# A Mamba-2 layer and a gated FFN: the FFN's row copy behind the next tile's tanh, and squares and an output projection at other places

## The chip, the cores and the metric

The kernel runs on one core of a Trainium2 chip. The metric is device microseconds of one launch, weights' preparation included: the median of three runs, and beside it one execution that was profiled.

## The reference

Input x is (4, 512, 512): four sequences ("batches") of 512 tokens. All weights are float32 inputs.

```
xn  = layernorm(x)
out = x + (xn + mamba2(xn)) + ffn(xn)

mamba2: z, xBC, dt = split(xn @ w_in)            # 1024, 1280, 16 columns
        xBC = silu(causal_conv4(xBC) + conv_b);  X, B, C = split(xBC)
        dt  = softplus(dt + dt_bias);  A = -exp(A_log)
        y   = ssd(X*dt, dt*A, B, C) + X*D        # state space, 16 heads of 64
        y   = y * silu(z)
        y   = y * rsqrt(mean(y*y) + eps) * norm_w
        return y @ w_out
ffn:    hidden = fwht(silu(xn @ W1.T) * (xn @ W3.T))   # 2048 wide, Hadamard
        return hidden @ W2.T
```

## The kernel before

**Precision.** Each product of the large projections is three float16 matmuls (high part by high part, high by low, low by high), summed in PSUM in float32. A weight tile is scaled by a power of two from its sum of squares and split into parts: ScalarE writes the high part (`split_hi`, line 924), VectorE the low part (`split_lo`, line 1194). In batch 0 this happens while the tiles are used, and the parts are stored to HBM; batches 1 to 3 load them.

**Tiles.** A batch has 50 weight tiles, each 12 matmuls of 128x512 on TensorE: ten C (conv inputs), eight Z (gate z), and sixteen pairs A(i), U(i), the FFN's gate and linear rows. For A, ScalarE takes a tanh from PSUM and VectorE makes `hs` from it (line 1260). For U, VectorE multiplies `hs` by the tile in PSUM (line 1265), ScalarE copies the result as float16 to `hid_hi` (line 978), and GpSimd subtracts that copy from `hs` for `hid_lo` (line 1443). After the tiles come sixteen steps G(i), which multiply hidden by W2; in batch 0 also H(i), which prepare W2.

**Quarters.** The state-space part runs over four quarters c of 128 tokens, as steps put between the tiles. T: transposes and the product B by C on TensorE; Xdt on VectorE (1339); on GpSimd x times D (`XD`, 1464) and Xdec (1468). ES: decay differences, on ScalarE (1059) for half of the heads, on GpSimd (1454, 1458) for the others. X: their exponentials on ScalarE (1072, 1074) and the product with `Gm` on VectorE (1348). S: state products on TensorE (782), the new state's matmul from Xdec (788), t1 on VectorE (1353), its sum with XD and the state's decay on GpSimd (1495, 1497). R: state sum on VectorE. Y: diagonal matmuls (796), y's sum and gate on VectorE (1365, 1368), and y's square with its row sum on ScalarE (1083). N, Q, V: scale, column sums and mean of y's squares; yh, yl. ROW: reciprocal root on GpSimd. W: output projection, 24 matmuls (line 600 with `wo_hi`, `wo_lo`), into PSUM bank 3 for quarters 0 to 2.

**Order.** There is one list per batch, `SCHEDULES[b]`, made by `make_schedule` from `FIRST`, `FIRST_AT` and `STEP_FIRST` for batch 0, and from `FRONT` and `STEP_AT` for the others. An entry of a step is the number of FFN tiles (A and U counted) that stand ahead of it. All five engines walk this one list and issue, in order, what their branch has for an item, so an engine that waits holds up all its later items. Copies, tanhs and products wait on semaphores of one count per tile or quarter.

**Weight scales in batch 0.** The FFN's weights are scaled in eight quads of four tiles. SQ takes the quad's squares on ScalarE in two halves (line 1008), QS sums them over the partitions on TensorE (739, 740, columns 2 and 3 of bank 3) and makes the scale on VectorE (`to_scale`, 1172 to 1178, 1308). WOQ, WOS and WOH are the same for w_out: squares (1033), sum and scale (644, 1330), high parts (1037) and low parts (1333). F transforms W2's blocks (719) and copies them out (1015).

The lines ahead of the change at its main place, on ScalarE:

```python
else:                                   # U
    if i == 0:
        act.wait_ge(w2_used.sem, w2_used.at(b, -1))
    act.wait_ge(evac.sem, evicted(b, key))
    nc.scalar.activation(hid_hi[:, i, :], hs[i % 2], ACT.Copy).then_inc(hid_h.sem, 1)
```

## Time and profile before

| | before |
|---|---|
| median of 3 runs (lowest, highest) | 968.58 us (967.49, 969.43) |
| profiled execution, its own time | 965.39 us |
| span from first to last instruction | 963.6 us |
| TensorE busy | 934.7 us, 97% |
| VectorE, ScalarE, GpSimd busy | 555.8, 391.4, 276.1 us |
| copy of U's rows, line 978 | 64 of 629 ns |
| subtract on GpSimd, line 1443 | 64 of 1113 ns |
| mean granted clock of TensorE | 0.996 of 2.4 GHz |
| chain that ended last | TensorE 67% |

TensorE's matmuls are pipelined: one of 128x512 in float16 is listed with 379 ns, but the next starts 0.216 us later, so a tile takes 2.6 us. An idle time is listed in front of the instruction that ended it, with the releaser that came last. Batch 0 lies before 301.6 us of the span, batch 1 before 522.6, batch 2 before 743.8.

### The profile page before, as it was taken

To read this page: it belongs to the slowest core of one execution; us is meant where nothing else is said; L and a number is where in the kernel's file an instruction comes from. 1 tells how busy PE (TensorE), PEld (TensorE's weight loads), DVE (VectorE), ACT (ScalarE), POOL (GpSimd) and SP (SyncE) were. 2 spreads that over 40 slices of the span, in tenths; PEclk is the share of its full clock that TensorE was granted. 3 is DMA by queue.
4 is the path that set the end of the run, shared out by engine and by line. 5 is a ranking of instruction groups with operands and counts; after the bars stand their busy time and mean duration, and the time that the engine had idled before them with its cause. 6 is when DMAs were issued, how large, how long until landed. Compare 5 with 4: busy or idle time off the path is not lost.

```text
span 963.6 us, 13435 instructions
## 1 busy us (share of the span) xinstructions
PE 934.7 (97%) x5000; PEld 469.3 (49%) x5000; DVE 555.8 (58%) x955; ACT 391.4 (41%) x690; POOL 276.1 (29%) x354
## 2 busy tenths in 40 slices
PE   9899987989899999999999999999999999999998
PEld 4444443545344445555454445555445445555543
DVE  7876588875534756556532766566451666575421
ACT  6678874533323445233221434233222444343200
POOL 0000446352000116466110106565210104654410
PEclk9999999999999999999999999999999999999999
DMA  9798355434224335525223435436223435256123
GB/s 336 247 349 295 112 192 193 131 124 137 96 74 147 125 111 159 155 72 176 88 67 113 143 99 164 145 97 175 78 76 101 143 107 160 65 151 153 45 77 98
DMA packets 76208, 134.26 MB, mean 139 GB/s; under 512 B 7536, under 2 KB 20464, under 8 KB 74096
## 3 DMA queue, kind: packets, MB, share of 16 engines
q1 hardware_dynamic: 56640, 104.88, 34.1%
q10 hardware_dynamic: 19504, 28.53, 10.0%
q8 instruction: 40, 0.66, 0.3%
q14 instruction: 24, 0.20, 0.1%
HBM read 107.43 MB, written 25.95 MB: 138 GB/s over the span
## 4 chain that ended last, share of the span: by engine, by line
PE 67%; DVE 1%; DMA 1%; ACT 1%; issue 0%; DVEq 0%; ACTq 0%
PE ps L600 46%; PE ps L834 14%; PE ps L796 2%; PE ps L782 1%; PE ps L788 1%; PE ps L768 1%; DMA arena<-cs_rows 1%; PE ps L619 0%; PE ps L638 0%; PE ps L751 0%; PE ps L771 0%; DVE arena L1348 0%; DVE arena L1426 0%; ACT arena L1059 0%; DVE arena L1265 0%
## 5 line engine op out<-in xcount | busy, mean ns | idle before, releaser
L600 PE MATMUL ps<-xh,arena 128*128 128x512 f16 x1592 | 487.9, 379 | 3.4 <-DVE arena L1194 3.3
L600 PE MATMUL ps<-xl,arena 128*128 128x512 f16 x796 | 302.0, 379 | 0.0
L600 PEld LDWEIGHTS ps<-xh,arena 128*128 128x128 f16 x1592 | 158.3, 99 | 190.3 <-issue 5.9
L834 PE MATMUL ps<-arena 128*128 128x512 f16 x768 | 171.1, 379 | 0.0
L1443 POOL TENSOR_TENSOR arena<-arena 128x512 f16<-128x512 f32 x64 | 71.2, 1113 | 334.6 <-ACT arena L978 334.6
L1244 DVE SCALAR_TENSOR_TENSOR arena<-ps,cw,arena 128x511 f32<-128x511 f32 (+2 forms) x120 | 89.4, 747 | 66.9 <-ACT arena L968 65.0
L600 PEld LDWEIGHTS ps<-xl,arena 128*128 128x128 f16 x796 | 77.9, 98 | 88.7 <-issue 3.3
L834 PEld LDWEIGHTS ps<-arena 128*128 128x128 f16 x768 | 74.1, 98 | 91.2 <-issue 5.5
L978 ACT ACTIVATE arena<-arena 128x512 f16<-128x512 f32 x64 | 40.2, 629 | 141.3 <-DVE arena L1265 141.3
L1260 DVE SCALAR_TENSOR_TENSOR arena<-arena,ps 128x512 f32<-128x512 f32 x64 | 44.0, 687 | 77.3 <-ACT arena L973 77.0
L600 PE MATMUL ps<-wo_hi,arena 128*128 128x512 f16 x256 | 79.9, 384 | 3.6 <-DVE wo_lo L1333 3.4
L973 ACT ACTIVATE arena<-ps,f 128x512 f32<-128x512 f32 x64 | 43.4, 678 | 85.0 <-PE ps L600 85.0
L1454 POOL TENSOR_TENSOR arena<-arena 128x1024 f32<-128x1024 f32 x16 | 30.7, 1920 | 112.5 <-DMA arena<-cs_rows 112.5
L1265 DVE SCALAR_TENSOR_TENSOR arena<-ps,arena 128x512 f32<-128x512 f32 x64 | 44.1, 689 | 24.6 <-PE ps L600 23.3
L1348 DVE TENSOR_TENSOR arena<-arena 128x2048 f32<-128x2048 f32 x16 | 40.5, 2528 | 19.9 <-ACT arena L1074 19.9
L600 PE MATMUL ps<-wo_lo,arena 128*128 128x512 f16 x128 | 49.3, 385 | 0.0
L600 PEld LDWEIGHTS ps<-wo_hi,arena 128*128 128x128 f16 x256 | 25.3, 99 | 37.1 <-DVE wo_lo L1333 3.9
L1059 ACT ACTIVATE arena<-arena 128x128 f32<-128x128 f32 x128 | 40.5, 389 | 5.8 <-DMA arena<-cs_rows 5.8
L1194 DVE SCALAR_TENSOR_TENSOR arena<-arena,scl 128x512 f16<-128x512 f32 x50 | 38.7, 778 | 5.8 <-ACT arena L924 5.8
L924 ACT ACTIVATE arena<-arena,scl 128x512 f16<-128x512 f32 x50 | 35.3, 711 | 12.8 <-DVE f L1308 5.9
L968 ACT ACTIVATE arena<-ps,cb,cw 128x512 f32<-128x512 f32 x40 | 30.8, 771 | 23.1 <-PE ps L600 22.1
L1426 DVE SCALAR_TENSOR_TENSOR arena<-ps,f_w,arena 128x512 f32<-128x512 f32 x16 | 10.9, 745 | 50.3 <-PE ps L834 50.3
(179 smaller groups left out, 1092.8 us busy)
## 6 DMA issues: line engine op xcount, KB each, us to landing
arena<-w_parts SPq DMA_DIRECT2D x198, 256.0 KB, 2.6
w_parts<-arena SPq DMA_DIRECT2D x66, 256.0 KB, 2.6
arena<-cs_rows ACTq DMA_DIRECT2D x16, 1024.0 KB, 5.7
arena<-w SPq DMA_DIRECT2D x24, 512.0 KB, 4.9
arena<-ecs_rows ACTq DMA_DIRECT2D x24, 256.0 KB, 6.9
arena<-x ACTq DMA_DIRECT2D x18, 256.0 KB, 3.4
w_mid<-arena SPq DMA_DIRECT2D x8, 512.0 KB, 3.5
arena<-w_mid SPq DMA_DIRECT2D x16, 256.0 KB, 2.6
```

The source lines that it names most:

```text
L600: ins = nc.tensor.matmul(out_ap, lhs(i, a), rhs(i, c), start=(i == 0 and s == 0), stop=(i == n - 1 and s == 2))
L834: ins = nc.tensor.matmul(bank(t), hw[a][:, i, t * P:(t + 1) * P], w2s[i % W2R][:, d, :], start=(i == 0 and s == 0), stop=(i == JF - 1 and ...
L924: nc.scalar.activation(part_hi[p % PARTS], raw_tile(p), ACT.Copy, scale=scl[:, n:n + 1]).then_inc(w_hi.sem, 1)
L973: nc.scalar.activation(slot, src, ACT.Tanh, scale=f_half[:, 0:1] if kind == "Z" else f_13[:, i // 2:i // 2 + 1]).then_inc(tanh_ok.sem, 1)
L978: nc.scalar.activation(hid_hi[:, i, :], hs[i % 2], ACT.Copy).then_inc(hid_h.sem, 1)
L1059: ins = nc.scalar.activation(Eb[:, h, :], csbc[:, h, :], ACT.Relu, scale=-1.0, bias=cs_s[:, c * NH + h:c * NH + h + 1])
L1194: nc.vector.scalar_tensor_tensor(out=part_lo[p % PARTS], in0=raw_tile(p), scalar=scl[:, n:n + 1], in1=part_hi[p % PARTS], op0=ALU.mult, op ...
L1244: ins = nc.vector.scalar_tensor_tensor(out=a[:, s:L], in0=src[:, 0:L - s], scalar=cw[:, i, TAPS - 1 - s:TAPS - s], in1=a[:, s:L], op0=ALU. ...
L1260: nc.vector.scalar_tensor_tensor(out=hs[i % 2], in0=tb[tanh[key] % 2], scalar=1.0, in1=src, op0=ALU.add, op1=ALU.mult).then_inc(evac.sem, 1)
L1265: nc.vector.scalar_tensor_tensor(out=hs[i % 2], in0=src, scalar=HID / (2 * XS * XS), in1=hs[i % 2], op0=ALU.mult, op1=ALU.mult).then_inc(e ...
L1348: nc.vector.tensor_tensor(Eb, Eb, Gm.unsqueeze(1).to_broadcast([P, NH, P]), ALU.mult).then_inc(m_ok.sem, 1)
L1443: nc.gpsimd.tensor_tensor(hid_lo[:, i, :], hs[i % 2], hid_hi[:, i, :], ALU.subtract).then_inc(hid_l.sem, 1)
```

## The change

1. ScalarE's copy of U(i) to `hid_hi` is no longer issued at U(i). It is issued at the next tile, behind that tile's tanh (or behind the conv's first product, if the tile is a C); the copy of the last U stands behind its own tile.
2. In batch 0 the halves of a quad's squares are two items, SQ 2q and SQ 2q+1, most of them at two tiles in a row; quad 6's sum QS moves from 20 to 18 FFN tiles.
3. y's square on ScalarE is an item of its own, YS. In batch 0 it stands a tile after Y for quarters 0, 1 and 3, and at Y's tile for quarter 2; in the others it stands where it was, right behind Y.
4. In batch 0, N and Q of quarter 1 move from 20 to 21 FFN tiles, W of quarter 0 from 18 to 19, so that QS of quad 6 and tile A9 now stand ahead of W0. QS 6 waits on TensorE for V0's read of the mean instead of W0's result, VectorE no longer waits for N1 there, and W0 waits for quad 6's scale (count 7 instead of 6), as both use bank 3.

```diff
-FIRST = ("... C5 F1 SQ0 Z4 F2 C6 F3 QS0 Z5 F4 C7 F5 SQ1 Z6 F6 Z7 F7 QS1 E0 A0").split()
+FIRST = ("... C5 F1 SQ0 Z4 SQ1 F2 C6 F3 QS0 Z5 F4 C7 F5 SQ2 Z6 SQ3 F6 Z7 F7 QS1 E0 A0").split()
...
-            [("SQ", 2, 1), ("QS", 2, 3), ("SQ", 3, 4), ("QS", 3, 7), ("SQ", 4, 8), ("QS", 4, 12), ("SQ", 5, 11), ("QS", 5, 14),
-             ("SQ", 6, 16), ("QS", 6, 20), ("SQ", 7, 20), ("QS", 7, 23)] +
+            [("SQ", n, at) for n, at in enumerate((1, 2, 4, 5, 7, 8, 11, 12, 15, 16, 19, 20), 4)] +
+            [("QS", q, at) for q, at in enumerate((3, 7, 12, 14, 18, 23), 2)] +
...
-              "Y": (9, 17, 26, 34), "N": (12, 20, 28, 37), "Q": (12, 20, 28, 37), "V": (14, 23, 30, 39), "W": (18, 25, 31, 41),
-              "ROW": (15, 24, 31, 40)}
+              "Y": (9, 17, 26, 34), "YS": (10, 18, 26, 35), "N": (12, 21, 28, 37),
+              "Q": (12, 21, 28, 37), "V": (14, 23, 30, 39), "W": (19, 25, 31, 41), "ROW": (15, 24, 31, 40)}
...
     "Y": (6, 14, 22, 32),
+    "YS": (6, 14, 22, 32),
...
                         elif i == 6:
-                            pe.wait_ge(mamba_evac.sem, mamba_evac.at(0, 0))
+                            pe.wait_ge(mean_read.sem, mean_read.at(0, 0))
...
                             pe.wait_ge(wo_l, QE)
-                            pe.wait_ge(scale_13, 6)
+                            pe.wait_ge(scale_13, 7)
...
+                def hidden_hi(key):
+                    i = key[1]
+                    if i == 0:
+                        act.wait_ge(w2_used.sem, w2_used.at(b, -1))
+                    act.wait_ge(evac.sem, evicted(b, key))
+                    nc.scalar.activation(hid_hi[:, i, :], hs[i % 2], ACT.Copy).then_inc(hid_h.sem, 1)
...
-                    else:
-                        if i == 0:
-                            act.wait_ge(w2_used.sem, w2_used.at(b, -1))
-                        act.wait_ge(evac.sem, evicted(b, key))
-                        nc.scalar.activation(hid_hi[:, i, :], hs[i % 2], ACT.Copy).then_inc(hid_h.sem, 1)
+                    if p > 0 and STREAMS[b][p - 1][0] == "U":
+                        hidden_hi(STREAMS[b][p - 1])
...
                         finish((kind, i))
+                        if POS[b][kind, i] == NT - 1:
+                            hidden_hi((kind, i))
...
-                    elif kind == "Y":
+                    elif kind == "YS":
...
-                        if i in (4, 6):
-                            dve.wait_ge(pe_tot.sem, pe_tot.at(0, i // 6))
+                        if i == 4:
+                            dve.wait_ge(pe_tot.sem, pe_tot.at(0, 0))
```

ScalarE's branch for SQ makes one half per item, with the same instruction on the same data as before.

## Rows read from the trace of the kernel before

**Rows 1.** The page, part 1: busy us, share of the span and instructions of each engine.

```profile
PE 934.7 (97%) x5000; PEld 469.3 (49%) x5000; DVE 555.8 (58%) x955; ACT 391.4 (41%) x690; POOL 276.1 (29%) x354
```

**Rows 2.** Busy time by batch: stretch, its us, then each engine, granted clock, DMA share, GB/s.

```profile
0.00:301.60 301.60, 276.32 (x1437) 137.55 (x1438) 200.96 (x398) 169.35 (x299) 71.65 (x96) 0.99 0.56 187
...
301.60:522.60 221.00, 221.00 (x1216) 112.11 (x1216) 121.51 (x198) 76.67 (x136) 68.67 (x87) 1.00 0.40 120
```

**Rows 3.** Timeline of TensorE: start, us, line, operands, then idle before it and its releaser.

```profile
45.08 0.39 PE L600 MATMUL ps<-xh,arena 128*128 128x512 f16 x1 [2.37 <-DVE arena L1194]
...
120.28 0.36 PE L644 MATMUL ps<-row_sq,con 128*128 128x9 f32 x2 [1.27 <-ACT arena L1033]
...
128.88 0.35 PE L739 MATMUL ps<-row_sq,con 128*128 128x2 f32 x2 [3.04 <-issue]
...
138.62 0.38 PE L810 MATMUL ps<-cmean,arena 128*128 128x1 f32 x2 [0.58 <-DVE arena L1372]
...
152.43 1.97 PE L796 MATMUL ps<-arena 128*64 128x128 f32 x32 [2.14 <-DVE arena L1353]
...
160.53 0.50 PE L600 MATMUL ps<-wo_hi,arena 128*128 128x512 f16 x1 [3.43 <-DVE wo_lo L1333]
...
172.59 0.28 PE L739 MATMUL ps<-row_sq,con 128*128 128x2 f32 x2
```

**Rows 4.** Busy time in stretches of 25 us, columns as in rows 2.

```profile
25.00:50.00 25.00, 21.59 (x147) 10.44 (x145) 21.03 (x38) 17.17 (x27) 1.11 (x3) 1.00 0.74 254
...
125.00:150.00 25.00, 21.38 (x107) 12.04 (x105) 21.97 (x48) 20.12 (x37) 13.33 (x12) 0.93 0.42 134
...
150.00:175.00 25.00, 19.43 (x115) 10.15 (x114) 18.59 (x23) 11.97 (x23) 13.54 (x15) 0.93 0.58 190
```

**Rows 5.** Timeline of GpSimd, step T0 of batch 1, then Xdec of batch 2.

```profile
357.62 1.09 POOL L1443 TENSOR_TENSOR arena<-arena 128x512 f16<-128x512 f32 x1 [16.97 <-ACT arena L978]
358.66 1.90 POOL L1464 TENSOR_TENSOR arena<-arena,dcol 128x1024 f32<-128x1024 f32 x1
361.46 1.90 POOL L1468 TENSOR_TENSOR arena<-arena 128x1024 f32<-128x1024 f32 x1 [0.89 <-DVE arena L1339]
...
582.42 1.90 POOL L1468 TENSOR_TENSOR arena<-arena 128x1024 f32<-128x1024 f32 x1 [0.89 <-DVE arena L1339]
```

**Rows 6.** Timeline of TensorE, batch 1: the state matmul.

```profile
364.96 1.88 PE L788 MATMUL ps<-arena 128*128 128x512 f32 x4
```

**Rows 7.** Timeline of ScalarE, batch 1: tanh of Z7.

```profile
358.83 0.69 ACT L973 ACTIVATE arena<-ps,f_half 128x512 f32<-128x512 f32 x1 [1.29 <-PE ps L600]
```

**Rows 8.** Timeline of VectorE, batch 1: product of step X0.

```profile
361.96 3.55 DVE L1348 TENSOR_TENSOR arena<-arena 128x2048 f32<-128x2048 f32 x1 [0.38 <-ACT arena L1074]
```

**Rows 9.** Two lines of VectorE: durations in ns (min/median/max), first and last start.

```profile
L1348 DVE TENSOR_TENSOR arena<-arena x16: 2282/2293/3552, 111.2 to 906.1; 128x2048 f32<-128x2048 f32 x16
...
L1333 DVE SCALAR_TENSOR_TENSOR wo_lo<-arena,nws,wo_hi x8: 739/747/2040, 134.0 to 159.7; 128x512 f16<-128x512 f32 x8
```

**Rows 10.** Timeline of VectorE and of GpSimd, batch 1, one after the other.

```profile
447.86 1.67 DVE L1387 SCALAR_TENSOR_TENSOR arena<-arena 128x1024 f16<-128x1024 f32 x1
...
448.40 2.88 POOL L1464 TENSOR_TENSOR arena<-arena,dcol 128x1024 f32<-128x1024 f32 x1
```

**Rows 11.** Timeline of ScalarE, batch 0: a square and the tanh of A2.

```profile
100.52 1.04 ACT L1008 ACTIVATE arena<-arena 128x1024 bf16<-128x1024 f32 x1
...
105.24 0.67 ACT L973 ACTIVATE arena<-ps,f 128x512 f32<-128x512 f32 x1
```

**Rows 12.** Timeline of TensorE, batch 0: the state matmul.

```profile
107.28 1.10 PE L788 MATMUL ps<-arena 128*128 128x512 f32 x2
```

**Rows 13.** Timelines of GpSimd, ScalarE and VectorE, batch 0, quarter 1.

```profile
134.28 2.34 POOL L1464 TENSOR_TENSOR arena<-arena,dcol 128x1024 f32<-128x1024 f32 x1
...
138.34 0.67 ACT L973 ACTIVATE arena<-ps,f 128x512 f32<-128x512 f32 x1
...
148.87 2.28 DVE L1348 TENSOR_TENSOR arena<-arena 128x2048 f32<-128x2048 f32 x1
```

More of the change, by code:

```diff
@@ L39 @@
 WARM = (32, 8)
-FIRST = ("B G1S C C0 G1N C1 Z0 DT C2 DTL Z1 C3 Z2 C4 SUM Z3 WOL F0 C5 F1 SQ0 Z4 F2 C6 F3 QS0 Z5 F4 C7 F5 SQ1 Z6 F6 Z7 F7 QS1 E0 A0").split()
+FIRST = ("B G1S C C0 G1N C1 Z0 DT C2 DTL Z1 C3 Z2 C4 SUM Z3 WOL F0 C5 F1 SQ0 Z4 SQ1 F2 C6 F3 QS0 Z5 F4 C7 F5 SQ2 Z6 SQ3 F6 Z7 F7 QS1 E0 A0").split()
 FRONT = "CZCCZCZeCZCZeCPCZCZCPZ"
@@ L997, in _ @@
                     elif kind == "SQ":
-                        act.wait_ge(d_quad[i], 32)
+                        quad, half_of = divmod(i, 2)
+                        act.wait_ge(d_quad[quad], 32)
                         if i == 0:
                             act.wait_ge(sq_g1, G1_ACT)
-                        elif i == QUADS_EARLY:
+                        elif i == 2 * QUADS_EARLY:
                             act.wait_ge(xt_done.sem, xt_done.at(0, MC - 1))
-                        junk = sq_act[i >= QUADS_EARLY]
-                        for half_of in range(2):
-                            if i not in (0, QUADS_EARLY):
-                                act.wait_ge(sq_quads, 2 * i + half_of - 1)
-                            column = SQ_Q + 2 * i + half_of
-                            nc.scalar.activation(junk[:, half_of * 2 * TILE:(half_of + 1) * 2 * TILE].rearrange("p (s c) -> p s c", s=2),
-                                                 raw_load_view(i, half_of), ACT.Square,
-                                                 accum_out=row_sq[:, column:column + 1]).then_inc(sq_quads, 1)
+                        if quad not in (0, QUADS_EARLY):
+                            act.wait_ge(sq_quads, i - 1)
+                        junk = sq_act[quad >= QUADS_EARLY][:, half_of * 2 * TILE:(half_of + 1) * 2 * TILE]
+                        nc.scalar.activation(junk.rearrange("p (s c) -> p s c", s=2), raw_load_view(quad, half_of), ACT.Square,
+                                             accum_out=row_sq[:, SQ_Q + i:SQ_Q + i + 1]).then_inc(sq_quads, 1)
                     elif kind == "F":
```

## The prediction

> **What bounds the kernel now.** Read the page's busy line first [rows 1]: TensorE is busy for 934.7 of 963.6 us, VectorE for 555.8, ScalarE and GpSimd for less. So the kernel is a queue of matmuls, and an edit on another engine counts only through TensorE's waits. The second view, busy time by batch [rows 2], says where those waits are: from 301.6 to 522.6, which is batch 1, TensorE is busy for all of 221.00 us (batches 2 and 3 repeat it), while in batch 0 it misses 25.3 us of 301.6. Two things follow. The change can gain only in batch 0; in batches 1 to 3, where the copy is deferred as well, it can only lose. The third view is TensorE's own timeline with the idle time ahead of an instruction [rows 3]: between 116 and 165 us it waits 1.27 us for a square of w_out (WOS), 3.04 for QS4, 0.58 for V0, 2.14 for Y1 and 3.43 for the output projection W0, 10.5 us in all. The granted clock is the fourth [rows 4]: the two stretches of 25 us that hold the 3.04 and the 3.43 us waits have a mean of 0.93, and the one with a 2.37 us wait at 45.08 has 1.00. Between the two levels, 2.4 and 1.2 GHz, a mean of 0.93 is 0.07 x 25 / 0.5 = 3.5 us at the lower one, so each of the two long waits cost 1.7 us more behind it.
>
> **The deferred copy: what it moves.** ScalarE's copy of a gated row block U(i) is now issued behind the next tile's tanh. That tile needs 12 matmuls, 2.6 us, so the copy comes some 2.5 us later, or more where steps stand between the two tiles. ScalarE itself loses nothing. But GpSimd takes its steps in order, and its subtract for U(i) waits for the copy; whatever is queued behind that subtract moves too. In every batch the steps behind U's are T (x times D, then Xdec), ES, ROW and S.
>
> **Batches 1 to 3, step T0.** Before, GpSimd runs the subtract of U1 at 357.62, XD at 358.66 and Xdec from 361.46 to 363.36 [rows 5]; the state matmul that needs Xdec starts at 364.96, without a wait [rows 6]. Now U1's copy comes behind Z7's tanh, which starts at 358.83 and takes 0.69 [rows 7]: the next instruction starts 0.1 before its end, at 359.4, the copy (0.63) ends at 360.05, subtract 360.1 to 361.2 (1.09), XD to 363.1 (1.90), Xdec to 365.0 (1.90). That alone is level with the 364.96 at which TensorE arrives: a loss of 0.0 to 0.1.
> It will not run so smoothly, because VectorE's product for step X0 falls into the same place. In the profile this product waits while Xdec runs: it starts at 361.96, half a microsecond into Xdec, and takes 3.55 us, where the median of its 16 instances is 2.29 [rows 8, 9]. The reverse is in [rows 10]: GpSimd's product, issued at 448.40 while VectorE's L1387 (two operands from SBUF) was running or first in line, took 2.88 instead of 1.90 and ended 1.75 us after L1387 did. So the two exclude each other for whole instructions, and the one that has been waiting goes next. Now ScalarE's exponentials end 0.2 us later (the copy is ahead of them), so the product is issued at 362.1 or 362.2, in the middle of XD (361.2 to 363.1). It gets its turn when XD ends and ends 2.15 us later, as it did behind Xdec (363.36 to 365.51): 365.25. Xdec, issued at 363.05, then waits for it and ends 1.75 later, at 367.0. The state matmul starts at 367.05 instead of 364.96: 2.1 us lost. Batch 2 repeats batch 1 to the hundredth (its Xdec is at 582.42, 220.96 later [rows 5]), and batch 3 likewise, so 3 x 2.1 = 6.3 us. Bounds: 0.0 a batch if there is no collision, 2.6 if a later margin (Xdec of quarter 2, which by the same working comes 0.5 us ahead of its matmul) is used up as well; I take 2.1, as 361.96 and 448.40 are the same two instruction kinds. A wait of 2.1 us is below the 2.37 that left the clock alone.
> The Trainium skill has this exclusion as a rule (SBUF — State Buffer, "Who interferes with whom"): a VectorE instruction with two SBUF inputs and a GpSimd one that reads SBUF hold the shared port for the whole instruction, in order of issue. By that rule the loss is 2.1 us a batch; without an exclusive lock it would be 0.1. The 3.55 us in [rows 8] agree with the rule.
> The rest of batches 1 to 3 I cost at nothing. S1 and S2 also stand behind a U, and their x*D sum arrives for Y1 and Y2 about 0.1 to 0.3 us later than TensorE's product, but N, which needs the result, comes two tiles later. The y square has only a new name there; it keeps its place on ScalarE.
>
> **Batch 0, step T0 (loss).** E0's transfer, whose issue doesn't move, gates ScalarE's first ES piece here, before and after. The copy of U1 stood ahead of two squares; it now stands behind the tanh of A2, which was at 105.24 [rows 11]. That tanh comes 1.04 earlier (one square has moved behind it) and another 0.54 (the copy has, less its 0.1 of overlap), at 103.66; tanh 0.57 and copy 0.62 give 104.85. Subtract, XD and Xdec, 4.9 us, end at 109.75, and VectorE's two weight splits hold them up by about 0.44 us each (what a VectorE instruction of that size cost XD at 134.28: 2.34 instead of 1.90 [rows 13]), up to 110.6. Before, the state matmul started at 107.28 [rows 12]. TensorE also gets there 0.2 later, since quad 2's second square now ends just behind A1. Loss 2.5 to 3.2; I take 3.2 (both splits do fall beside GpSimd's work). A 3.2 us wait lies with the two that dropped the clock, not with the 2.37: 1.7 more. Sum +4.9.
>
> **Batch 0, WOS and QS4 (gain).** At WOS the last w_out square stood behind U3's copy, which waited for VectorE; now nothing stands there: -1.4 (1.27 idle and 0.14 around it). At QS4 TensorE waited for VectorE's w_out scale, which was late because ScalarE stood in front of y's square, waiting for the gate, before it made the split that VectorE needs ahead of that scale. With that square a tile later the split runs ahead of it; by my count the scale is there about 3 us before QS4. -3.2, and the low clock behind it, -1.7. Sum -6.3. What is late next is V0: y's column sums come 1.0 us after TensorE instead of 0.58: +0.4.
> So TensorE is at V0 1.0 us earlier than before (4.9 - 6.3 + 0.4).
>
> **Batch 0, quarter 1 (loss).** U5's copy now waits for yh (behind N0), a split and A6's tanh, which was at 138.34. So T1's subtract, XD (at 134.28 before) and Xdec (1.90 more, to 138.5, clear of all but the first of VectorE's w_out low parts) fall beside a split and two of those parts [rows 13]. Such a part took 2.04 at worst, beside a GpSimd product, where its median is 0.75 [rows 9]. Two such collisions (1.3 each) and a subtract's 0.45, less 0.5 of idle that VectorE had: X1's product, at 148.87 before, comes 2.7 later against V0, so Y1, which waits for it and for t1, comes 1.7 later than its 152.43. Bounds: no collision, 0; all three in full, 4.1.
>
> **Batch 0, W0.** Before, from Y1 at 152.43 to QS6 at 172.59 there are 20.2 us [rows 3]: Y1, U8, the wait, W0 at low clock, A9, U9. Now QS6 and A9 come ahead of W0, which waits for QS6's scale. Counted from X1's product, by the spacing of starts: the product and t1 3.3, three tiles 1.8, three splits and two w_out parts 3.3, y's sum and gate 2.45, the scale 0.75, 11.6 in all, and two waits for the port behind S1's products, 1.7 each: 15.0, an estimate. W0 (5.2) follows. X1's product (148.87) to the end of W0 and A9, a tile before 172.59, was 21.1 us; it becomes 20.3, or 22.0 if this wait of about 4 us drops the clock as 3.43 did. QS6's own 0.36 us is inside now, and was not. I take -0.3. Behind W0 are only U9 and T2 on TensorE; the row transfer for T2 on ScalarE's queue waits for W0's result, which comes a tile ahead.
> Batch 0 in all: -1.0 + 2.7 - 0.3 = +1.4.
>
> **Edits at nothing.** Splitting quads 0 and 1 between the F steps: the F copies keep their times, as the square that left one place came back in front of the next tile's copy. QS6's wait on V0 instead of W0, and VectorE's dropped wait for N1, are met long before. No transfer is added; the parts' stores and raw loads on the SP queue hang on VectorE's splits and move with them, and GpSimd issues none.
>
> **Sum.** 6.3 + 1.4 = +7.7 on the profiled execution's 965.4 us (span 963.6 and 1.8 around it), 973.1. The median of the runs, 968.6, is 3.2 higher; I put the same 7.7 on it: 976.3.
>
> **Rivals.**
> 1. Faster: Xdec gets the port straight behind XD in batches 1 to 3 (0.1 a batch), and batch 0 keeps its WOS and QS4 gain with neither the clock drop at T0 nor the quarter-1 collisions. It decides at one point: whether VectorE's product is issued before XD ends. 0.3 + (3.2 - 6.3 + 0.4 - 0.3) = -2.7: 965.9. For it: the subtract could start earlier than I have it only if the copy did, and 358.83 forbids that. Against it: [rows 8, 10]. Chance 8%.
> 2. The port costs 2.1 a batch, but quarter 1 in batch 0 has no collision and T0 no clock drop: 6.3 - 3.0 = +3.3, 971.9. For it: the order of VectorE and GpSimd there hangs on tenths. Chance 27%; its lower third lies within 0.2% of 968.6.
> 3. All waits of batch 0 drop the clock and all collisions come in full: 6.3 + 4.9 - 6.3 + 0.4 + 4.1 + 0.5 = +9.9, 978.5 (the 0.5 is 22.0 for 21.1 at W0, less QS6's 0.36). Chance 15%.
> The forecast, 974 to 978, has 50%.
> A difference of 0.2%, about 1.9 us, is what a measurement of this kernel can tell from none. Faster 8% (rival 1), same 9% (the low end of rival 2), slower 83%. Range 970 to 981: it leaves out rival 1, the low end of rival 2 and the top of rival 3.
>
> **What would show it.** Right: in each of batches 1 to 3 one wait of about 2 us ahead of the first L788 after T0, with GpSimd's L1468 the releaser and 3.5 to 4 us long; busy time there down by it. In batch 0 a wait of about 3 us ahead of that matmul too, WOS and QS4 without waits, a longer one at Y1 or W0. Wrong: batches 1 to 3 still full, or batch 0 shorter by over 5 us.

## The result, and the profile after

The changed kernel takes 992.08 us (median of 4 runs, 989.23 to 992.79), the kernel before beside it 968.04 (4 runs). The ratio is 1.0248, 95% interval 1.0215 to 1.0281: slower by 24 us, where +7.7 was forecast and 981 was the upper end of the range. The sign was right, the size was not. The profiled execution took 991.81, its span is 990.0, which is 26.4 over the 963.6 of before.

The page's busy line of the changed kernel:

```profile
span 990.0 us, 13439 instructions
PE 945.7 (96%) x4999; PEld 473.8 (48%) x5000; DVE 573.0 (58%) x955; ACT 388.1 (39%) x690; POOL 296.5 (30%) x354
```

Against [rows 1] ScalarE is busy 3 us less, VectorE 17 and GpSimd 20 us more, with as many instructions of each: they take longer beside each other, as the port rows below show for two of them. By batch (columns: stretch, its length, busy time of each engine, granted clock, DMA share, GB/s):

```profile
0.00:317.19 317.19, 282.57 (x1428) 140.32 (x1429) 211.27 (x396) 168.39 (x297) 77.86 (x96) 0.96 0.53 177
317.19:542.22 225.03, 222.76 (x1216) 112.90 (x1215) 123.35 (x199) 75.59 (x135) 73.23 (x87) 0.99 0.39 118
542.22:765.34 223.12, 221.13 (x1215) 112.05 (x1214) 123.39 (x199) 75.57 (x135) 73.24 (x87) 1.00 0.39 119
765.34:990.00 224.66, 219.28 (x1145) 108.56 (x1144) 115.03 (x164) 68.54 (x123) 72.16 (x84) 0.99 0.38 112
```

The cuts here are at the matmuls of the cumulative sums, with which each batch ends on TensorE (300.61, 521.56 and 742.78 in the kernel before). Batch 0 lost 16.6 us (317.19 for 300.61), the others 4.1, 1.9 and 3.8, together 9.8. Of batch 1's 225.03 TensorE is busy for 222.76, where [rows 2] had it busy throughout. The waits of TensorE that answer to [rows 3] (start, length, instruction, and in brackets the idle time ahead of it and who ended it):

```profile
111.57 0.87 PE L789 MATMUL ps<-arena 128*128 128x512 f32 x1 [3.37 <-POOL arena L1473]
...
138.20 0.27 PE L811 MATMUL ps<-cmean,arena 128*128 128x1 f32 x1 [0.63 <-DVE arena L1377]
...
144.98 0.70 PE L789 MATMUL ps<-arena 128*128 128x512 f32 x1 [2.00 <-POOL arena L1473]
...
156.19 0.80 PE L797 MATMUL ps<-arena 128*64 128x128 f32 x5 [2.35 <-DVE arena L1358]
...
167.55 0.38 PE L601 MATMUL ps<-wo_hi,arena 128*128 128x512 f16 x1 [2.08 <-issue]
...
214.93 0.58 PE L808 MATMUL ps<-arena,con 128*128 128x1 f32 x2 [6.11 <-ACT arena L1088]
...
266.31 0.59 PE L808 MATMUL ps<-arena,con 128*128 128x1 f32 x2 [5.89 <-ACT arena L1088]
...
383.98 1.10 PE L789 MATMUL ps<-arena 128*128 128x512 f32 x2 [2.27 <-POOL arena L1473]
```

The waits at WOS and QS4 are gone. In their place T0 waits 3.37, and S1 2.00; Y1 still waits 2.35 and W0 2.08. At 214.93 and 266.31 stand two waits of six microseconds each, ahead of N2 and N3. Neither is in the prediction. Both are for the square of y on ScalarE (L1088; the changed kernel's line numbers are a few higher than those of the kernel before).

Both are followed back on ScalarE (first fence), and from there on VectorE and GpSimd (second and third):

```profile
197.07 1.27 ACTq L1055 DMA_DIRECT2D arena<-ecs_rows  x2
198.47 0.72 ACT L925 ACTIVATE arena<-arena,scl 128x512 f16<-128x512 f32 x1 [8.54 <-issue]
199.10 0.67 ACT L981 ACTIVATE arena<-ps,f 128x512 f32<-128x512 f32 x1
199.66 0.62 ACT L960 ACTIVATE arena<-arena 128x512 f16<-128x512 f32 x1
...
213.73 1.06 ACT L1088 ACTIVATE arena<-arena 128x1024 f32<-128x1024 f32 x1 [12.83 <-DVE arena L1373]
...
262.29 2.93 ACT L854 ACTIVATE arena<-arena 128x512 f32<-128x512 f32 x4 [6.35 <-DVE arena L1136]
265.13 1.04 ACT L1088 ACTIVATE arena<-arena 128x1024 f32<-128x1024 f32 x1
```

```profile
210.02 1.22 DVE L1363 TENSOR_TENSOR arena<-ps,arena 128x1024 f32<-128x1024 f32 x1 [1.86 <-POOL arena L1502]
...
250.27 1.28 DVE L1373 SCALAR_TENSOR_TENSOR arena<-arena,f_half 128x1024 f32<-128x1024 f32 x1
```

```profile
200.36 1.09 POOL L1448 TENSOR_TENSOR arena<-arena 128x512 f16<-128x512 f32 x1 [11.77 <-ACT arena L960]
...
205.25 2.35 POOL L1500 TENSOR_TENSOR arena<-arena 128x1024 f32<-128x1024 f32 x1
207.56 2.35 POOL L1502 TENSOR_TENSOR arena<-arena 128x1024 f32<-128x1024 f32 x1
```

N2: U11's copy (199.66) stands behind A12's tanh, and that behind step E3, whose DMA issue (197.07) waits until VectorE has made t1 (197.04). ScalarE computes nothing for 8.54 us. GpSimd has been idle for 11.77 when it gets the copy; then it does the subtract, ROW1 (twelve tiny steps) and the two products of S2, and VectorE's L1363 waits for the last of them; y's sum, the gate and the square follow.

N3: the gate (last row of the second fence) is done at 251.55, but the square starts at 265.13. Ahead of it on ScalarE stand the four normalizations of LN1, which wait for VectorE until 262.29.

In batch 1 GpSimd's Xdec takes 3.95 us, and VectorE's product, issued at 378.99 while XD ran, 3.08; in [rows 5] Xdec takes 1.90, and the median of the product is 2.29 [rows 9]:

```profile
378.02 1.90 POOL L1469 TENSOR_TENSOR arena<-arena,dcol 128x1024 f32<-128x1024 f32 x1
379.88 3.95 POOL L1473 TENSOR_TENSOR arena<-arena 128x1024 f32<-128x1024 f32 x1
```

```profile
378.99 3.08 DVE L1353 TENSOR_TENSOR arena<-arena 128x2048 f32<-128x2048 f32 x1 [0.55 <-ACT arena L1079]
```

### The profile page after: what moved, and what is told of

Same layout as the page of the kernel before. It is cut to its first block, busy times and chain, and to the rows that moved or that the text cites. A ratio compares the mean times of both kernels' runs of the same rounds, so it can differ in the third digit from the quotient of the medians.

```text
span 990.0 us, 13439 instructions
## 1 busy us (share of the span) xinstructions
PE 945.7 (96%) x4999; PEld 473.8 (48%) x5000; DVE 573.0 (58%) x955; ACT 388.1 (39%) x690; POOL 296.5 (30%) x354
## 4 chain that ended last, share of the span: by engine, by line
PE 61%; issue 5%; POOL 2%; DVE 0%; ACT 0%; DVEq 0%; POOLq 0%
PE ps L601 39%; PE ps L835 14%; PE ps L797 2%; PE ps L789 2%; PE ps L783 2%; POOL arena L1473 1%; PE ps L769 1%; POOL arena L1448 1%; POOL arena L1469 1%; PE ps L620 0%; PE ps L639 0%; PE ps L752 0%; DVE arena L1431 0%; PE ps L772 0%; ACT arena L960 0%
## 5 line engine op out<-in xcount | busy, mean ns | idle before, releaser
L1448 POOL TENSOR_TENSOR arena<-arena 128x512 f16<-128x512 f32 x64 | 77.0, 1203 | 383.1 <-ACT arena L960 383.1
L835 PE MATMUL ps<-arena 128*128 128x512 f16 x768 | 173.6, 382 | 0.0
L1199 DVE SCALAR_TENSOR_TENSOR arena<-arena,scl 128x512 f16<-128x512 f32 x50 | 47.6, 956 | 2.5 <-ACT arena L925 2.3
L1088 ACT ACTIVATE arena<-arena 128x1024 f32<-128x1024 f32 x16 | 16.9, 1056 | 81.0 <-DVE arena L1373 81.0
```

The lines of the kernel that those rows point to most:

```text
L835: ins = nc.tensor.matmul(bank(t), hw[a][:, i, t * P:(t + 1) * P], w2s[i % W2R][:, d, :], start=(i == 0 and s == 0), stop=(i == JF - 1 and ...
L1199: nc.vector.scalar_tensor_tensor(out=part_lo[p % PARTS], in0=raw_tile(p), scalar=scl[:, n:n + 1], in1=part_hi[p % PARTS], op0=ALU.mult, op ...
L1448: nc.gpsimd.tensor_tensor(hid_lo[:, i, :], hs[i % 2], hid_hi[:, i, :], ALU.subtract).then_inc(hid_l.sem, 1)
```

## Experiments

Each kernel was timed in five rounds against the kernel before on the same chip; ratios are to that kernel, with 95% intervals. The changed kernel stands at 1.0248, known to 3.2 us either way; 0.01 in a ratio is 9.7 us. The code shows pieces of lines, and `...` stands for what is left out between them. `at_once(b, i)` names the U copies that stand at their own tile again; where an edit of the changed kernel doesn't show it, all 64 stay deferred.

**1. Quarter 3's square ahead of LN1.**

```
-"YS": (10, 18, 26, 35)
+"YS": (10, 18, 26, 34)
```

> The changed kernel with one number put back: the square of y for quarter 3 of batch 0 stands at place 34, ahead of ScalarE's normalization of the next batch's x (LN1), as y's gate did before, where the change has it at 35, behind LN1. Theory A (the order on ScalarE alone makes TensorE's 5.89 us wait ahead of N3 at 266.31 of the changed kernel): in that profile the gate is done at 251.55 and the square starts only at 265.13, so the wait goes, and the low clock behind it (265.5 to 272.3, 6.8 us at half speed, so 3.4 us) with it: -9.3, about 983 us, and no wait over 1 us ahead of N3. Rival B (quarter 3 is late as a whole, because the deferred copies hold GpSimd and VectorE up, and the order only hides that): the wait stays over 3 us, gain under 4 us, 988 us or more.

Measured: 982.00 us, 1.0157 (1.0139 to 1.0174), 8.8 us less than the changed kernel by the ratios. The square now starts right behind the gate, ahead of LN1 (L854), and TensorE has no wait at N3:

```profile
249.03 1.06 ACT L1088 ACTIVATE arena<-arena 128x1024 f32<-128x1024 f32 x1 [3.80 <-DVE arena L1373]
...
259.79 2.93 ACT L854 ACTIVATE arena<-arena 128x512 f32<-128x512 f32 x4 [6.34 <-DVE arena L1136]
```

Theory A holds: one place in a list cost about 9 us.

**2. U11's copy back, batch 0.**

```
+def at_once(b, i):
+    return b == 0 and i == 11
...
-if p > 0 and STREAMS[b][p - 1][0] == "U":
+if p > 0 and STREAMS[b][p - 1][0] == "U" and not at_once(b, STREAMS[b][p - 1][1]):
     hidden_hi(STREAMS[b][p - 1])
...
-if POS[b][kind, i] == NT - 1:
+if kind == "U" and (at_once(b, i) or POS[b][kind, i] == NT - 1):
     hidden_hi((kind, i))
```

> The changed kernel, with one of its 64 deferred copies put back: the copy of U11 in batch 0 stands at U11 again, ahead of step E3, whose DMA issue on ScalarE waits for VectorE's t1. Theory A (the copy held behind that wait makes the 6.11 us wait ahead of N2 at 214.93): the copy comes at about 190, GpSimd's subtract and ROW1 are over before t1 (197.04), S2 starts there and ends at 201.8 instead of 209.9; the wait ahead of N2 falls below 1 us and the low clock of 212.0 to 221.1 (9.1 us at half speed, 4.5) goes: -6 to -10.6, less a wait of up to 2.3 that H0 may get back; about 983 us. Rival B (t1 itself is 3.6 us later than before the change, since VectorE's X2 product is at 189.75 and not at 185.34, and this is what makes y late): a wait of 3 us or more stays ahead of N2, gain under 4 us, 988 us or more.

Measured: 988.85 (986.64 to 993.49), 1.0233 (1.0206 to 1.0260). That is only 1.5 under the changed kernel, and the intervals overlap. GpSimd's subtract is early again, and S2 starts at 200.75 instead of 205.25, but 2.48 us stay ahead of N2:

```profile
196.50 1.09 POOL L1451 TENSOR_TENSOR arena<-arena 128x512 f16<-128x512 f32 x1 [6.46 <-ACT arena L963]
...
200.75 2.35 POOL L1503 TENSOR_TENSOR arena<-arena 128x1024 f32<-128x1024 f32 x1
203.07 2.35 POOL L1505 TENSOR_TENSOR arena<-arena 128x1024 f32<-128x1024 f32 x1
```

So both theories were half right. From N1 to N2 TensorE takes 32.17 us instead of 35.82. H0, a little later, waits 1.54 again (2.31 in the kernel before, none in the changed one), but that took nothing back: from N2 to N3 both kernels take 51.4. The 3.65 don't show in the medians: the six runs lie between 986.64 and 993.49, and the intervals tell the gain neither from none nor from 3.65.

**3. U1's copy back, batches 1 to 3.**

```
+    return b > 0 and i == 1
```

> The changed kernel, with the copy of U1 in batches 1, 2 and 3 (three copies) back at U1, ahead of the next tile's tanh. Theory A (these three copies make all that batches 1 to 3 lost): the waits of 2.27, 1.99 and 1.99 us ahead of the first state matmul go, the low clock behind two of them too, the three batches are back at about 221 us each: -9.8, about 982 us. Rival B (another deferred copy of these batches, U5, U9 or U13, fills part of the gap with a wait of its own once TensorE is 2 us earlier): gain 3 to 7 us, 985 to 989, with new waits at S1 to S3 or at N.

Measured: 983.12, 1.0167 (1.0150 to 1.0183), 7.8 us less. The three waits are gone and no other came in these batches. Theory A holds. The size is 2 under the 9.8 of the one profiled execution; the intervals do not tell the two apart, and the clock does not always fall behind these waits (the clock rows behind experiment 16).

**4. Only the deferral, on the kernel before.**

```
+if p > 0 and STREAMS[b][p - 1][0] == "U":
+    hidden_hi(STREAMS[b][p - 1])
```

(the copy taken out of its own tile, as in the change; no other edit.)

> The kernel before with one part of the change alone: all 64 copies of U behind the next tile's tanh; squares, y's square and the output projection stay where they were. Theory A (the deferral alone costs more than the whole change shows, and the other parts give some back): batches 1 to 3 lose 9.8 us as in the changed kernel, T0 and N2 of batch 0 lose about 5 and 9, WOS gives 1.4 back, N3 has no wait: about +20, 988 us. Rival B (the deferral costs only what batches 1 to 3 and T0 lose, and N2's wait comes from the other parts of the change, which make t1 late): +13 to +15, 981 to 983 us, with a wait below 2 us ahead of N2.

Measured: 985.24, 1.0186 (1.0169 to 1.0204), +18.0. The wait ahead of N2 is 6.34, at N3 there is none. Theory A, 2 to 3 us less than it said. The deferral alone makes about three quarters of the loss. It also takes the wait at QS4 away, though y's square stands where it stood: behind a longer wait at T0 TensorE comes to QS4 at 132.69, where in the kernel before it waited from 125.84 to 128.88.

```profile
112.94 1.19 PE L788 MATMUL ps<-arena 128*128 128x512 f32 x1 [5.15 <-POOL arena L1474]
...
132.69 0.28 PE L739 MATMUL ps<-row_sq,con 128*128 128x2 f32 x2
```

**5. Everything but the deferral.**

```
+    return True
...
-"YS": (10, 18, 26, 35)
+"YS": (10, 18, 26, 34)
```

> The changed kernel with all 64 copies of U back at their own tile, and the square of y for quarter 3 ahead of LN1: what is left of the change is squares a half at a time, y's square a tile later in quarters 0 and 1, and the output projection W0 behind QS6. Theory A (the deferral and quarter 3's order are all that costs, and the rest is a gain as the prediction had it for QS4, V0 and W0: -3.2 -1.7 +0.4 -0.3): batches 1 to 3 at 221 us, N2 without a wait over 0.5, 1.27 us at WOS as before, 4 to 6 us under the kernel before, about 962. Rival B (QS4's gain hung on the deferral too, or y's square a tile later gives it back at V0, N1 or N2): within 2 us of the kernel before, 965 to 969.

Measured: 971.62, 1.0046 (1.0029 to 1.0062): slower by 4.4. Both theories fail. What the prediction saw as the gain of the change is a loss without the deferral (experiment 8 finds it in W0's place). TensorE's timeline in this kernel shows it at QS5, W0 and N2:

```profile
136.68 0.56 PE L740 MATMUL ps<-row_sq,con 128*128 128x2 f32 x2 [2.60 <-issue]
...
164.83 0.58 PE L601 MATMUL ps<-wo_hi,arena 128*128 128x512 f16 x1 [4.73 <-issue]
...
211.13 0.38 PE L808 MATMUL ps<-arena,con 128*128 128x1 f32 x2 [2.18 <-ACT arena L1091]
```

**6. VectorE's product held until Xdec is done, batches 1 to 3** (on the changed kernel, step X on VectorE).

```
 dve.wait_ge(gm_ok.sem, gm_ok.at(b, c))
+if b > 0 and c == 0:
+    dve.wait_ge(xdec_ok.sem, xdec_ok.at(b, c))
```

> The changed kernel with one wait more: in batches 1, 2 and 3 VectorE's product of step X0 waits until GpSimd's Xdec of T0 is done. Theory A (the state matmul is late because that product, issued at 378.99 during XD, gets the port ahead of Xdec, which then takes 3.95 us instead of 1.90): Xdec takes 1.90 again and ends at about 381.8, TensorE's wait of 2.27, 1.99 and 1.99 us there falls to 0.0 to 0.2; the product ends at about 384.1, and Y0 waits for it 0 to 0.8 us. A gain of 4 to 6, and 3.5 more for the low clock behind two of the waits: 981 to 987 us. Rival B (the copy, 2.5 us later, is reason enough, and the port adds nothing): the wait before the state matmul stays at 1.9 to 2.3, and Y0 waits too: 991 us or more.

Measured: 985.33, 1.0178 (1.0161 to 1.0196), 6.8 us less. Xdec takes 1.91 again, though the copy is as late as in the changed kernel; the state matmul does not wait, and Y0 waits 0.38 in each of the three batches:

```profile
380.10 1.91 POOL L1475 TENSOR_TENSOR arena<-arena 128x1024 f32<-128x1024 f32 x1
```

Theory A: the lateness of the copy was nearly harmless by itself, the order in which two engines got one port cost 2 us a batch. The Trainium skill's rule (SBUF — State Buffer, "Who interferes with whom"), a lock on the shared port for a whole instruction, agrees with 3.95 against 1.91.

**7. As 5, with U3's copy in batch 0 deferred.**

```
+    return not (b == 0 and i == 3)
```

> As the kernel with all copies at their own tile and the square of y for quarter 3 ahead of LN1, but with one copy deferred, that of U3 in batch 0, where the prediction had a gain (WOS, whose last square of w_out stands behind this copy). Theory A: WOS's 1.27 us goes and nothing else moves: 1 to 2 us under that kernel, about 961. Rival B (the square of w_out is late for another reason, or TensorE loses the time again at Y0 or N0): within 0.7 us of that kernel.

Measured: 969.95, 1.0022 (1.0008 to 1.0037), 1.7 under experiment 5 by the medians; the intervals overlap. The expected reason is not it: WOS has no wait in experiment 5 either. It is inconclusive.

**8. As 5, with W0 ahead of QS6 again.**

```
-("QS", q, at) for q, at in enumerate((3, 7, 12, 14, 18, 23), 2)
+("QS", q, at) for q, at in enumerate((3, 7, 12, 14, 20, 23), 2)
...
-"N": (12, 21, 28, 37), "Q": (12, 21, 28, 37), "W": (19, 25, 31, 41)
+"N": (12, 20, 28, 37), "Q": (12, 20, 28, 37), "W": (18, 25, 31, 41)
...
-pe.wait_ge(scale_13, 7)
+pe.wait_ge(scale_13, 6)
```

(The waits of QS6 are put back likewise.)

> As the kernel with all copies at their own tile and the square of y for quarter 3 ahead of LN1, and besides with the output projection W0 ahead of QS6, and N1 a tile earlier, as in the kernel before; left of the change are the squares a half at a time and y's square a tile later in quarters 0 and 1. Theory A (by the prediction W0 behind QS6 is worth -0.3): within 1 us of that kernel. Rival B (W0 behind QS6 takes a wait of 3.43 us and its low clock away): 3 to 5 us above that kernel, with a wait of 2 to 4 us ahead of W0. Rival C (W0 behind QS6 costs, since W0 then waits for VectorE's whole chain to QS6's scale): 1 to 4 us under that kernel.

Measured: 966.24, 0.9990 (0.9975 to 1.0005), 5.4 under experiment 5. W0 waits 3.22 for the last low part of w_out instead of 4.73 for QS6's scale, and N2's 2.18 falls to 0.43. Rival C, and more than it said.

```profile
161.53 0.61 PE L601 MATMUL ps<-wo_hi,arena 128*128 128x512 f16 x1 [3.22 <-DVE wo_lo L1341]
```

**9. As 8, with W0 one tile later.**

```
-"W": (18, 25, 31, 41)
+"W": (19, 25, 31, 41)
```

> As the kernel with all copies at their own tile, the square of y for quarter 3 ahead of LN1 and W0 ahead of QS6, but with W0 one tile later (behind A9 instead of U8), still ahead of QS6. In the kernel with W0 at U8 the last low part of w_out is ready at 161.47, and TensorE waits 3.22 us for it. Theory A (a tile of 2.6 us fills that wait, and a wait of 0.6 leaves the clock alone): 2.6 to 4.3 us under the kernel with W0 at U8, 962 to 964. Rival B (QS6, right behind W0 now, has to wait until VectorE has read W0's result: the wait only moves): a wait of 2 us or more at QS6 and no gain.

Measured: 965.79, 0.9976 (0.9960 to 0.9993). W0 waits 0.37, but QS6 behind it 1.58, both theories in part; the intervals do not tell it from experiment 8:

```profile
160.73 0.39 PE L601 MATMUL ps<-wo_hi,arena 128*128 128x512 f16 x1 [0.37 <-DVE wo_lo L1341]
...
170.25 0.35 PE L740 MATMUL ps<-row_sq,con 128*128 128x2 f32 x2 [1.58 <-issue]
```

**10. The changed kernel, with W0 ahead of QS6 again** (the edit of 8, alone).

> The changed kernel, deferral and all, with W0 ahead of QS6 and N1 a tile earlier, as in the kernel before. Theory A (what W0 behind QS6 cost without the deferral, 5 us, it costs in the changed kernel as well): about 986 us. Rival B (in the changed kernel TensorE comes to W0 so late that the order there hardly matters; N2's wait stays, since U11's copy alone makes it): 989 to 993 us, with the wait ahead of N2 still about 6 us.

Measured: 990.29 (985.20 to 992.30), 1.0223 (1.0195 to 1.0251): no difference from the changed kernel that the intervals could tell. Rival B; the wait ahead of N2 is 6.37.

**11. The kernel before, with W0 one tile later** (the edit of 9).

> The kernel before with one number changed: W0 one tile later (behind A9 instead of U8), still ahead of QS6. In the profile before TensorE waits 3.43 us there for the last low part of w_out, and the low clock behind it took 1.7 more. Theory A (the tile fills the wait): 2.6 to 4.3 us under the kernel before, about 963. Rival B (QS6 right behind W0 waits for VectorE to read W0's result): no gain.

Measured: 967.51, 1.0000 (0.9981 to 1.0020). Rival B: W0's wait is 0.84 instead of 3.43, and QS6's is 2.64 instead of none:

```profile
171.30 0.24 PE L739 MATMUL ps<-row_sq,con 128*128 128x2 f32 x1 [2.64 <-issue]
```

**12. As 9, with U3's copy in batch 0 deferred** (the edit of 7).

> As the kernel with W0 one tile later, ahead of QS6, squares a half at a time and y's square a tile later in quarters 0 and 1, and besides the copy of U3 in batch 0 deferred, the one deferred copy that did not cost. Theory A (the parts add up: 1 us from the halves and the squares, 2.6 to 4.3 from W0, up to 1.5 from U3): 960 to 964 us. Rival B (VectorE bounds this stretch, and what is won at one wait comes back at the next): not under 965.

Measured: 964.59 (963.80 to 966.11), 0.9967 (0.9953 to 0.9981). Just above theory A's 960 to 964, and under the 965 of rival B. With experiment 9 it is one of two versions whose intervals lie under the kernel before, this one by 3.2 us; the two are not told apart by their intervals. Of the change it keeps the squares a half at a time, y's square a tile later in quarters 0 and 1, W0 a tile later, and one deferred copy of 64.

**13. U11's copy and W0 put back together** (the edits of 2 and 8).

> The changed kernel with U11's copy in batch 0 back at its own tile, and W0 ahead of QS6 and N1 a tile earlier as in the kernel before; 63 copies stay deferred. Theory A (the 6.1 us wait ahead of N2 has two causes side by side, U11's copy at 6.1 to 6.4 and the late X2 product behind W0's new place at 2.2 to 2.7, and the longer one shows): with both gone the wait is under 0.6 us; about 984 us. Rival B (the rest of the wait comes from the deferral elsewhere, U5 or U7, which makes VectorE late): 2 us or more stay, 987 us or more.

Measured: 987.88 (983.32 to 988.94), 1.0185 (1.0156 to 1.0215). 2.73 stay ahead of N2: theory A is refuted, rival B stands, though for another copy than those it named. GpSimd's and VectorE's rows of this kernel show what else is late:

```profile
183.08 2.34 POOL L1472 TENSOR_TENSOR arena<-arena,dcol 128x1024 f32<-128x1024 f32 x1
185.38 2.35 POOL L1476 TENSOR_TENSOR arena<-arena 128x1024 f32<-128x1024 f32 x1
```

```profile
184.19 1.78 DVE L1202 SCALAR_TENSOR_TENSOR arena<-arena,scl 128x512 f16<-128x512 f32 x1
...
186.49 1.79 DVE L1202 SCALAR_TENSOR_TENSOR arena<-arena,scl 128x512 f16<-128x512 f32 x1
...
188.90 2.48 DVE L1356 TENSOR_TENSOR arena<-arena 128x2048 f32<-128x2048 f32 x1
```

U9's copy, deferred past N1's work and A10's tanh, puts T2's XD and Xdec beside VectorE's weight splits. Each delays the other, and the product for X2 starts at 188.90.

**14. The causes found so far put back** (with the edits of 1 and 8).

```
+    return (b == 0 and i == 11) or (b > 0 and i == 1)
```

> The changed kernel with all the causes found put back: quarter 3's square of y ahead of LN1, U11's copy in batch 0 and U1's in batches 1 to 3 at their own tile, W0 ahead of QS6; 60 copies stay deferred. Theory A (these are all that it lost, but for T0, S1 and Y1 of batch 0, some 7 us with their low clock, against the waits at WOS, QS4 and V0 that are gone): 966 to 970 us. Rival B (a further loss hides behind them and comes up once they are gone): 973 us or more, with a wait of over 2 us at a place that had none.

Measured: 969.60, 1.0008 (0.9993 to 1.0022): theory A. Of the 2.48% of the changed kernel nothing is left that can be told from zero, with 60 copies still deferred. 2.73 us stay ahead of N2.

**15. U9's and U11's copies back.**

```
+    return b == 0 and i in (9, 11)
```

> The changed kernel with two copies of batch 0, U9's and U11's, back at their own tile; W0 stays behind QS6. Theory A (U9's copy makes GpSimd's T2 collide with VectorE's splits, and so X2's product and t1 late): XD and Xdec of T2 end before 182, the splits beside them take 0.75 again, and the wait ahead of N2, 2.65 with U11 alone, falls to 0.4 to 2.2 (2.2 is what W0 behind QS6 left without any deferral): about 984 us. Rival B (W0's place or U5's copy makes them late): 2.6 us or more stay ahead of N2.

Measured: 987.36, 1.0219 (1.0191 to 1.0248). T2's Xdec ends at 179.46, but the wait ahead of N2 is 2.51: as good as what U11 alone left (2.48, not the 2.65 of the expectation). With W0 behind QS6 a second cause is there (2.18 in experiment 5, where no copy is deferred), which the next run lacks.

**16. As 14, with U9's copy back too.**

```
+    return (b == 0 and i in (9, 11)) or (b > 0 and i == 1)
```

> The changed kernel with quarter 3's square of y ahead of LN1, U9's and U11's copies in batch 0 and U1's in batches 1 to 3 at their own tile, W0 ahead of QS6; 59 copies stay deferred. Against the kernel with the same repairs but U9's. Theory A: the wait ahead of N2 falls from 2.72 to about 0.4 and the low clock behind it goes: 2.3 to 4 us less, 965 to 967.5. Rival B (T2's lateness is used up elsewhere): the wait stays over 2 us, 969 us or more.

Measured: 969.20, 1.0019 (1.0000 to 1.0038). T2's Xdec ends at 183.17, and VectorE's three splits from 182.97 on take 0.75, 0.74 and 1.60, where they took 1.60, 1.78 and 1.79 in experiment 13. One of them:

```profile
181.26 1.91 POOL L1476 TENSOR_TENSOR arena<-arena 128x1024 f32<-128x1024 f32 x1
```

```profile
184.24 0.74 DVE L1202 SCALAR_TENSOR_TENSOR arena<-arena,scl 128x512 f16<-128x512 f32 x1
```

The wait ahead of N2 falls from 2.73 to 1.24, not to 0.4, and H0 behind it waits 3.17 instead of 1.47, with a clock of 0.79 over the next 8 us. So N1 to N2 is 1.80 shorter, and N2 to N3 is 1.69 longer (47.07 for 45.38). The collision is gone, the time is not: rival B for the time. What the last 0.8 us at N2 hang on stays open.

**The clock behind one and the same wait**, over 8 us from the state matmul of T0 in batches 1, 2, 3 on, after waits of 1.99 to 2.27 (the granted clock is the third number from the end). The changed kernel, then that of experiment 1:

```profile
384.00:392.00 8.00, 8.00 (x49) 4.47 (x50) 2.45 (x2) 1.02 (x1) 0.00 (x0) 0.79 0.49 175
608.80:616.80 8.00, 8.00 (x62) 4.96 (x63) 2.51 (x2) 2.61 (x4) 0.00 (x0) 1.00 0.65 195
831.90:839.90 8.00, 8.00 (x49) 3.97 (x50) 2.46 (x2) 1.02 (x1) 0.00 (x0) 0.79 0.36 143
```

```profile
373.80:381.80 8.00, 8.00 (x62) 4.97 (x63) 2.51 (x2) 2.64 (x4) 0.00 (x0) 1.00 0.58 186
596.90:604.90 8.00, 8.00 (x49) 4.07 (x50) 2.49 (x2) 1.02 (x1) 0.00 (x0) 0.79 0.46 151
...
```

A mean of 0.79 is 0.21 x 8 / 0.5 = 3.4 us at 1.2 GHz, which costs 1.7. In the changed kernel and experiments 1, 2 and 4 together the clock fell behind 6 of the 12 such waits, and in experiments 10, 13 and 15, which have them too, behind 7 of 9. The same batch is at 0.79 in one execution and at 1.00 in another.

The same holds of the wait of 2.37 at 45.08 [rows 3], from which the prediction took its bound. Every kernel here has it, and in 7 of the 18 profiled executions (experiments 2, 3, 9, 10, 12, 14 and 16) the clock is at 0.79 behind it. From experiment 2:

```profile
45.09 0.39 PE L601 MATMUL ps<-xh,arena 128*128 128x512 f16 x1 [2.36 <-DVE arena L1202]
...
45.09:53.09 8.00, 8.00 (x36) 4.01 (x37) 7.75 (x16) 6.25 (x14) 0.00 (x0) 0.79 0.90 302
```

## Why the prediction was right in sign and wrong in size

By its own landmarks (start before, start after; difference from before):

| step | before | after | difference | predicted |
|---|---|---|---|---|
| T0, state matmul | 107.28 | 111.57 | +4.29 | +3.2 |
| V0 | 138.62 | 138.20 | -0.42 | -1.0 |
| Y1 | 152.43 | 156.19 | +3.76 | +1.7 |
| T2 | 172.95 | 175.32 | +2.37 | +1.4 |
| N2 | 206.89 | 214.93 | +8.04 | +1.4 |
| N3 | 251.43 | 266.31 | +14.88 | +1.4 |
| end of batch 0 (sums) | 300.61 | 317.19 | +16.58 | +1.4 |
| batches 1 to 3 | | | +9.8 | +6.3 |

**Batches 1 to 3, the wait: right.** The collision that was read out of [rows 5, 8, 10] came as worked out: waits of 2.27, 1.99 and 1.99, 6.25 for 6.3, an Xdec of 3.95, and the port as its cause (experiments 3 and 6). **The clock behind it: wrong.** "A wait of 2.1 us is below the 2.37 that left the clock alone" took one instance in [rows 3, 4] for a bound; that same wait is followed by the low clock in 7 of 18 executions. Behind two of the three waits the clock fell, +3.5 in this execution. Experiment 3 puts wait and clock together at 7.8, within its interval of this execution's 9.8.

**T0 of batch 0: right.** 3.2 us plus a drop of the clock were forecast; 3.37 and a drop came. TensorE itself also comes there 0.9 later, where 0.2 was counted.

**WOS, QS4, V0: right in sum by luck, not in reason.** From T0's start to V0's TensorE won 4.7 us (4.29 + 0.42), where 4.2 were forecast (6.3 less 0.4 and less the 1.7 of T0's clock). But without the deferral these edits win 1 us, which the interval does not tell from nothing (experiment 8), QS4 waits 2.19 there (3.04 in the kernel before) and QS5 0.91. In the changed kernel VectorE has the w_out scale at 127.97, only 0.8 earlier than before, but TensorE comes to QS4 at 130.15 instead of 125.84, behind its wait at T0. So most of the gain at QS4 was that loss, seen from the other end; with the deferral alone, y's square unmoved, QS4 does not wait either (experiment 4).

**Quarter 1: right in place, too small.** 4.2 lost from V0 to Y1 for 2.7, just over the upper bound of 4.1: X1's product came at 152.62, 14.4 behind V0 instead of 10.25. The prediction's own terms add up to 2.55 (two collisions of 1.3, 0.45, less 0.5), not 2.7; what it took too small is the collision. Two of VectorE's w_out parts, before and after, beside T1's subtract, XD and Xdec (in which the split ahead of them took 1.60 instead of 0.75):

```profile
140.31 1.41 DVE L1333 SCALAR_TENSOR_TENSOR wo_lo<-arena,nws,wo_hi 128x512 f16<-128x512 f32 x2
...
140.78 4.69 DVE L1338 SCALAR_TENSOR_TENSOR wo_lo<-arena,nws,wo_hi 128x512 f16<-128x512 f32 x2
```

They lost 3.28 together and the split 0.85, 4.1 in all, and none of VectorE's idle time took it up. S1's state matmul waited 2.00 for Xdec as well, for which the prediction had no term.

**W0: small in the changed kernel, as forecast, and that by luck** (-0.3; 1.4 won from Y1 to T2; experiment 10 finds nothing). Without the deferral the same edit costs 5.4 (experiments 5 and 8). The chain from X1's product to QS6's scale, counted at 15.0, took 14.8 (152.62 to 167.44), as worked out; but W0's wait for it is 2.08 in the changed kernel and 4.73 without the deferral, since TensorE comes to it behind the losses ahead.

**Behind T2: the step that failed.** 14.2 of the 16.6 us that batch 0 lost lie there, and the prediction costed them at nothing. Its sentence was "Behind W0 are only U9 and T2 on TensorE", and it then summed the batch. It had itself said that the steps behind U's are T, ES, ROW and S in every batch, but it worked that out for U1 and U5 and not for U9 (T2) and U11 (ROW1, S2, behind E3's wait): +5.67 at N2. Experiment 4 shows that the deferral alone makes as much. In four kernels with W0 ahead of QS6 the stretch from N1 to N2 tells the copies apart:

| copies of batch 0 deferred | experiment | N1 | N2 | N1 to N2 |
|---|---|---|---|---|
| none | 8 | 176.43 | 209.15 | 32.72 |
| all but U9's and U11's | 16 | 176.19 | 209.72 | 33.53 |
| all but U11's | 14 | 174.07 | 209.40 | 35.33 |
| all | 10 | 174.05 | 213.02 | 38.97 |

U11's copy makes 3.64 of the 6.25 and U9's 1.80; 0.81 stays open. In the changed kernel W0 behind QS6 holds N2 up by itself as well (2.18 in experiment 5), and there U9's copy gave nothing back (2.51 in experiment 15 for 2.48 in experiment 2).

The other part, +6.84 at N3 and +1.70 more up to the sums, is nearly all the move of y's square in quarter 3 from 34 to 35, behind LN1, for which the prediction has no term. With that one entry put back (experiment 1) N2 to N3 takes 45.39 instead of 51.38, and N3 to the sums 49.16 instead of 50.88: 7.7 of the 8.5 us. The other 0.85 (N2 to N3 took 44.54 before) is there with the deferral alone too, 45.39 in experiment 4. For a moved step, what sorts between its old place and its new one has to be read off the list: here it was ScalarE's four normalizations, waiting for VectorE.

The range had been made from the bounds of the steps that were worked out. It held nothing for those that were not.

## What to carry to other kernels

An edit that applies to every instance of a loop has to be costed at every instance whose neighbours differ; here one of 64 copies (U11's, 3.6) and one entry of a list (7.7) made two thirds of the 16.6 us that batch 0 lost. An in-order engine turns "a little later" into "behind whatever waits next": for each moved instruction, look for the first wait that stands between its old place and its new one. And a gain at a wait that lies behind a loss of the same size is not yet a gain: take the loss away and see whether it stays.

## What the runs showed of the hardware

Waits of TensorE of 1.99 to 2.27 us ahead of T0's state matmul were followed by the low clock (1.2 GHz for about 3.4 us) in 13 of 21 cases, and one of 2.37, at the same place of every kernel, in 7 of 18, though not in the kernel before. The wait of 2.31 at H0 is followed by a clock of 1.00 in the kernel before and in experiment 11, and of 0.79 in experiments 8, 9 and 12. The length of a single wait does not tell whether the clock falls; by these cases a wait of about 2 us is priced at itself plus half of 1.7 us.

The kernel before ran from 963.92 to 971.07 us in the 29 runs beside experiments 9 to 12, 7 us. Drops of the clock are at most a part of that: the runs of 970.05 and 970.11 had a mean clock of 0.995, and the one of 963.92 had 0.994. What the rest is stays open.
